# Moving two steps of the output path of a groupnorm-attention kernel: VectorE's block transpose from slot 1 to slot 5, GpSimd's residual add from slot 5 to slot 7

## The chip, the cores and the metric

The kernel runs on one core of a Trainium2 chip. The metric is the device time of one execution in microseconds (us). Before the change it is 1938.38 us, the median of 3 runs (1937.92 to 1938.48).

## What is computed

For each of 4 images x of 256 channels by 4096 positions:

```python
xn   = groupnorm(x)                       # 32 groups of 8 channels, no weights
f, g = Wq @ xn, Wk @ xn                   # 64 x 4096 each
h    = Wv @ xn                            # 256 x 4096
beta = softmax(f.T @ g, axis=0)           # 4096 x 4096, over the rows n
out  = x + gamma[0] * (h @ beta) + xn     # the residual is x + xn
```

## The kernel before, in words

**Stages and slots.** The columns of the softmax matrix are worked off in chunks of 256: 16 chunks an image (CPB), 64 in all (K). One chunk is one stage k of the main loops. Its 4096 rows are 8 groups of 1024, and each group is one slot g. Every engine has its own copy of the loop over `n = 8k + g` (lines 410, 560, 677 and 938), with its part of each slot written out in program order; an engine only ever waits on semaphores, and everything behind a waiting instruction on that engine waits too. j is the number of the stage within its image, 0 to 15.

**A slot.** TensorE, on every second slot, first computes the scores of two groups of the chunk two stages ahead (`scores`, line 456, placed by `SCORES_AT`, line 61), then the 24 matmuls of `weigh` (line 483) that multiply the exponentials PH and PL of this slot with V into the output banks O. ScalarE copies scores to SC (`store`, line 607) and takes exponentials (`exps`, line 616). VectorE keeps running maxima (`maximum`, line 765) and subtracts them from the scores four slots ahead (`subtract`, line 818). GpSimd computes PL, the low half of the exponentials, three slots ahead (`low_weights`, line 375).

**The output path of a chunk.** In slot 0 of the next stage VectorE divides and scales the finished output (`divide`, `scale_output`, lines 845 and 851) into OSB. In slot 1, `turn_blocks` (line 859) transposes OSB in 32 by 32 blocks into OT. The SyncE queue, SP, waits for that in `regroup` (line 270) and issues 16 DMAs that move the blocks to ATT. In slot 5, GpSimd's `add_attention` (line 390) waits for all 16 to land and adds ATT to the residual RES, which `residual` (line 379) made in slot 4. Then SP stores the chunk (line 268).

**The order on SP.** SP works one list in order. For stage k (line 305) it holds: `regroup(k - 1)`; in stage 13 of an image (j == FG_FIRST + 1) six `move_f` and four `double_g` for the next image; in stage 14 `move_f` of unit 7; `store(k - 1)`, which waits for the add; `residual_input(k + 1)`; in some stages an xin load of 1 MB (line 281), with which VectorE later works in slots 3 and 5 (bn_stats in stages 1 to 4, `normalise` in stages 7 to 10); in stage 13 the last `move_f` and three `double_g`. `move_f(u)` (line 283) copies a unit of f and g of the next image into F1 with two DMAs (lines 290, 291), and `double_g(u)` (line 293) copies g into the other half of GG with one (line 297).

**Who needs the moves.** TensorE computes the scores of the next image's first chunk in stage 14. It waits for them in slots 0, 2, 4 and 6 (lines 568 to 572):

```python
                    if i == 0:
                        pe.wait_ge(f_in[q % G], 32 * (nb + 1))
                        pe.wait_ge(f_in[q % G + 1], 32 * (nb + 1))
                    if q % G == 0 and i % 2 == 0:
                        pe.wait_ge(g_in[i // 2], 16 * (nb + 1))
```

So slot 0 needs units 0 and 1 and the doubled unit 0, slot 6 needs units 6 and 7. There are three such changes of image.

Of the kernel before, what the change touches and what calls it, by code (L numbers as in the profile page):

```python
# [5 lines left out]
def groupnorm_attention(nc, x, wqT, wkT, wvT, gamma, out):  # L6
# [66 lines left out]
    with ExitStack() as ctx:  # L73
# [275 lines left out]
        def _(pool):  # L349
# [25 lines left out]
            def low_weights(s):  # L375
                pool.wait_ge(exp_done, s + 1)
                pool.tensor_tensor(PL[:, s % RING, :], sc(s), PH[:, s % RING, :], ALU.subtract).then_inc(pl_ready, 1)  # L377

            def residual(k):
                b = k // CPB  # L380
                pool.wait_ge(res_coefs, b + 1)
                pool.wait_ge(xres_in, 16 * (k + 1))
                if k >= 2:
                    pool.wait_ge(out_stored[k % 2], 16 * (k // 2))
                for h in range(H):
                    r = pool.tensor_scalar(RES[:, k % 2, h, :], xres[:, h, :], rscale[:, b % 2, h:h + 1],
                                           rbias[:, b % 2, h:h + 1], ALU.mult, ALU.add)
                r.then_inc(res_ready, 1)

            def add_attention(k):  # L390
                for q in range(NQ):
                    pool.wait_ge(att_in[q], 16 * NQ * (k + 1))
                pool.wait_ge(res_ready, k + 1)
                flat = "p h m q n -> p (h m q n)"
                r = RES[:, k % 2, :, :].rearrange("p h n -> p (h n)")
                pool.tensor_tensor(r, r, ATT[:, :, :, :, :].rearrange(flat), ALU.add).then_inc(out_ready, 1)  # L396

            def low_input(b, p):
                for h in range(H):
                    pool.wait_ge(xh_ready, H * NFG + H * (NPC * (b - 1) + p) + h + 1)  # L400
                    pool.tensor_tensor(XL[:, h, piece(p)], xin[:, h, :], XH[:, h, piece(p)],
                                       ALU.subtract).then_inc(xl_ready[h], 2)
# [7 lines left out]
            for n in range(K * G):  # L410
                k, g = divmod(n, G)
                b, j = divmod(k, CPB)
                if n + EXP_LEAD < K * G:
                    low_weights(n + EXP_LEAD)
                if g == 4:
                    residual(k)
                if g == 5 and k > 0:
                    add_attention(k - 1)
                if g == 6 and b + 1 < BATCH and NORM_FIRST <= j < NORM_FIRST + NPC:
                    low_input(b + 1, j - NORM_FIRST)  # L420
# [276 lines left out]
        def _(dve):  # L697
# [64 lines left out]
            def normalise(buf, h):  # L762
                return ve.tensor_scalar(buf, buf, nmean[:, h:h + 1], nrstd[:, h:h + 1], ALU.subtract, ALU.mult)

            def maximum(q):

                c, g = divmod(q, G)
                scores = S[:, q % 2, :]  # L770
                dve.wait_ge(s_ready, q + 1)
                if g == 0:
                    return
                if g == 1:
                    dve.wait_ge(s_stored, q)
                    if c > 0:
                        dve.wait_ge(mx_turned, c)
                    ve.tensor_tensor(XM[:, :], scores, sc(q - 1), ALU.max).then_inc(s_maxed, 2)  # L778
                    return
                if q % 2 == 0:  # L780
                    dve.wait_ge(s_stored, q + 1)
                dve.wait_ge(s_maxed, q + 1 if q % 2 == 0 else q - 1)
                ve.tensor_tensor(XM[:, :], scores, XM[:, :], ALU.max).then_inc(s_maxed, 1)  # L783

            def turn_maxima(c):
                dve.wait_ge(s_maxed, G * (c + 1))
                if c > 0:
                    dve.wait_ge(mxq_ready, c)
                ve.transpose(MT[:, :], XM[:, :]).then_inc(mx_turned, 1)
# [14 lines left out]
            def column_maxima(c, o):  # L804

                dve.wait_ge(mx_shared, c + 1)
                if c > 0:
                    dve.wait_ge(mb_ready, c)
                ve.tensor_reduce(mxc[:, :], o[:, 0:NQ * NB].rearrange("p (i j) -> p j i", i=NQ), axis=AX.X,
                                 op=ALU.max).then_inc(mxc_ready, 1)  # L810
# [7 lines left out]
            def subtract(s):  # L818
                k = s // G
                dve.wait_ge(mb_ready, k + 1)  # L820
                dve.wait_ge(s_stored, s + 1)
                tile = sc(s).rearrange("p (i m) -> p i m", i=GT)
                ve.tensor_tensor(tile, tile, MB[:, 0:M].unsqueeze(1).to_broadcast([P, GT, M]),  # L823
                                 ALU.subtract).then_inc(sub_ready, 1)
# [20 lines left out]
            def divide(k):  # L845
                dve.wait_ge(weighed, (k + 1) * G)
                for m in range(MB2):
                    r = ve.reciprocal(rden[:, m:m + 1], bank(k, m)[:, C:C + 1])
                r.then_inc(rden_ready, 1)

            def scale_output(k):
                dve.wait_ge(rden_ready, k + 1)
                if k > 0:
                    dve.wait_ge(osb_turned, k)
                for m in range(MB2):
                    ve.tensor_scalar(OSB[:, m, :], bank(k, m)[:, 0:C], rden[:, m:m + 1], gam[:, :],  # L856
                                     ALU.mult, ALU.mult).then_inc(osb_ready, 1)
# [80 lines left out]
            for n in range(K * G):  # L938
                k, g = divmod(n, G)
                b, j = divmod(k, CPB)  # L940
                if g == 0 and k > 0:
                    divide(k - 1)
                    scale_output(k - 1)
                q = SCORES_AT.get(n)
                if q is not None:
                    maximum(q + 1)
                if k > 0 and n + SUB_LEAD < K * G:
                    subtract(n + SUB_LEAD)
                if q is not None:
                    maximum(q)  # L950
                if n == 2:
                    turn_maxima(1)
                    subtract(6)
                    subtract(7)
                    quadrant_maxima(1)
                if n == 4:
                    column_maxima(1, shared0)
                    spread_maxima(1)
                if k == 0:
                    for s in FIRST_SUB[g]:  # L960
                        subtract(s)
                if g == 7 and k + 2 < K:
                    turn_maxima(k + 2)
                if g == 1 and k > 0:
                    turn_blocks(k - 1)
                if g == 1 and 0 < k < K - 1:
                    quadrant_maxima(k + 1)
                if g == 3 and 0 < k < K - 1:
                    column_maxima(k + 1, S[:, 0, :])
                    spread_maxima(k + 1)  # L970
                extra(k, g, MID)
                extra(k, g, END)
                if g in (3, 5) and b + 1 < BATCH:
                    part = g // 2 - 1
                    if STAT_FIRST <= j < STAT_FIRST + NPC:
                        p = j - STAT_FIRST
                        dve.wait_ge(xin_in, 16 * (2 * NPC * b + p + 1))
                        for h in range(H):
                            last = ve.bn_stats(stats[:, h, 2 * p + part, :], xin[:, h, part * 512:(part + 1) * 512])
                        if part == 1:  # L980
                            last.then_inc(xin_read, 1)
                    if NORM_FIRST <= j < NORM_FIRST + NPC:
                        p = j - NORM_FIRST
                        dve.wait_ge(xin_in, 16 * (2 * NPC * b + NPC + p + 1))
                        normalise(xin[:, part, :], part).then_inc(xn_ready, 1)
                if b + 1 < BATCH:
                    if (j, g) == (COEFS_AT, 3):
                        dve.wait_ge(xin_read, (b + 1) * NPC)
                        group_means(b + 1)
                    if (j, g) == (COEFS_AT, 5):  # L990
                        group_variances(b + 1)
                    if (j, g) == (COEFS_AT, 7):
                        guess_roots(b + 1)
                    if (j, g) == (COEFS_AT + 1, 3):
                        finish_roots(b + 1)
                    if (j, g) == (COEFS_AT + 1, 5):
                        spread_coefficients(b + 1)
# [26 lines left out]
```

## Time and profile before

| what | value |
|---|---|
| median of 3 runs | 1938.38 us |
| the profiled execution's own time | 1938.83 us |
| span of its instructions | 1937.0 us |
| TensorE matmuls busy | 1890.4 us (98% of the span) |
| VectorE, ScalarE, GpSimd busy | 1589.5, 1571.4, 1305.3 us |
| mean granted TensorE clock | 0.999 of 2.4 GHz |

The profiled execution takes 1.83 us beyond its span, and 0.45 us more than the median. Times in the trace count from the start of the span. Durations of matmuls overlap, since they are pipelined: the spacing of their starts is their cost.

### The profile page before, as it was taken

How to read it: one execution, taken by the hardware profiler on the slowest of the kernel's cores; microseconds unless marked ns; L12 is line 12 of the kernel's file. 1: busy time of each engine (PE TensorE's matmuls, PEld its weight loads, DVE VectorE, ACT ScalarE, POOL GpSimd, SP SyncE). 2: the span in 40 equal slices, each digit the busy share in tenths (PEclk: the TensorE clock that was granted, in tenths of full speed). 3: DMA queues.
4: the chain of work that ended last, by engine and by line, in shares of the span. 5: the costliest groups of instructions: out<-in, count | busy, mean ns of one | idle time of the engine just before them, and what ended most of it. 6: DMA issues, size and time to landing. Idle time of an engine off the chain costs nothing. (4 is left out here: it accounts for less than half of the span.)

```text
span 1937.0 us, 44170 instructions
## 1 busy us (share of the span) xinstructions
PE 1890.4 (98%) x17476; PEld 1562.9 (81%) x17476; DVE 1589.5 (82%) x1932; ACT 1571.4 (81%) x1677; POOL 1305.3 (67%) x761
## 2 busy tenths in 40 slices
PE   5999999999999999999999999999999999999998
PEld 3678888878878888887887888888788888888887
DVE  7888998877768899987876889998777787888784
ACT  4788889977768888897876888898787788888885
POOL 4367668866646677886654776788565577766777
PEclk9999999999999999999999999999999999999999
DMA  4022112212111211211211211121130011111111
GB/s 143 4 67 77 45 33 74 55 23 67 29 46 49 74 53 29 72 53 31 60 35 39 78 45 54 53 55 45 28 78 18 21 31 33 31 26 31 32 34 34
DMA packets 199021, 91.18 MB, mean 47 GB/s; under 512 B 150176, under 2 KB 191392, under 8 KB 198816
## 3 DMA queue, kind: packets, MB, share of 16 engines
q1 hardware_dynamic: 198816, 88.36, 17.4%
q8 instruction: 139, 2.28, 0.5%
q14 instruction: 66, 0.54, 0.1%
HBM read 46.60 MB, written 16.78 MB: 33 GB/s over the span
## 5 line engine op out<-in xcount | busy, mean ns | idle before, releaser
L377 POOL TENSOR_TENSOR PL<-SC,PH 128x1024 f16<-128x1024 f32 x511 | 1088.8, 2137 | 572.2 <-ACT SC L621 568.1
L492 PE MATMUL O<-V,PH 128*128 128x257 f16 x4096 | 1119.1, 273 | 4.3 <-DVE OSB L856 3.1
L494 PE MATMUL O<-V,PL 128*128 128x257 f16 x4096 | 1119.0, 273 | 0.0
L493 PE MATMUL O<-V,PH 128*128 128x256 f16 x4096 | 1117.2, 273 | 0.0
L620 ACT ACTIVATE PH<-SC 128x1024 f16<-128x1024 f32 x511 | 539.1, 1055 | 123.1 <-PE O L494 116.8
L823 DVE TENSOR_TENSOR SC<-SC,MB 128x1024 f32<-128x1024 f32 x511 | 613.6, 1211 | 0.1
L614 ACT ACTIVATE SC<-S 128x1024 f32<-128x1024 f32 x512 | 502.0, 1012 | 115.4 <-issue 102.0
L783 DVE TENSOR_TENSOR XM<-S,XM 128x1024 f32<-128x1024 f32 x384 | 468.4, 1220 | 127.4 <-PE S L480 126.1
L621 ACT ACTIVATE SC<-SC 128x1024 f32<-128x1024 f32 x511 | 533.0, 1043 | 0.0
L492 PEld LDWEIGHTS O<-V,PH 128*128 128x128 f16 x4096 | 406.3, 99 | 53.9 <-DVE OSB L856 4.4
L493 PEld LDWEIGHTS O<-V,PH 128*128 128x128 f16 x4096 | 401.1, 98 | 50.2
L494 PEld LDWEIGHTS O<-V,PL 128*128 128x128 f16 x4096 | 401.0, 98 | 50.1
L474 PE MATMUL S<-GG,F 128*128 128x256 f16 x1024 | 154.3, 273 | 6.1 <-ACT SC L614 2.5
L480 PE MATMUL S<-GG,F 128*128 128x256 f16 x1024 | 156.4, 275 | 0.0
L477 PE MATMUL S<-GG,F 64*128 64x256 f16 x2048 | 156.3, 272 | 0.0
L778 DVE TENSOR_TENSOR XM<-S,SC 128x1024 f32<-128x1024 f32 x64 | 78.4, 1224 | 87.3 <-ACT SC L614 87.2
L480 PEld LDWEIGHTS S<-GG,F 128*128 128x128 f16 x1024 | 79.2, 98 | 59.9 <-issue 54.0
L477 PEld LDWEIGHTS S<-GG,F 64*128 64x128 f16 x2048 | 79.1, 94 | 59.8 <-issue 53.9
L474 PEld LDWEIGHTS S<-GG,F 128*128 128x128 f16 x1024 | 98.9, 98 | 24.1 <-issue 6.5
L834 DVE TENSOR_TENSOR V<-O,V 128x512 f16<-128x512 f32 x62 | 42.4, 689 | 59.3 <-ACT V L631 59.0
L631 ACT CAST V<-O 128x512 f16<-128x512 f32 x62 | 35.9, 586 | 61.9 <-PE O L453 61.6
L396 POOL TENSOR_TENSOR RES<-RES,ATT 128x512 f32<-128x512 f32 x63 | 80.5, 1278 | 0.4 <-DMA ATT<-OT 0.4
(106 smaller groups left out, 1100.8 us busy)
## 6 DMA issues: line engine op xcount, KB each, us to landing
xin<-x SPq DMA_DIRECT2D x24, 1024.0 KB, 5.6
xres<-x SPq DMA_DIRECT2D x64, 256.0 KB, 2.8
out<-RES SPq DMA_DIRECT2D x64, 256.0 KB, 2.2
ATT<-OT SPq DMA_DIRECT2D x1008, 16.0 KB, 1.9
F<-GG SPq DMA_DIRECT2D x64, 64.0 KB, 2.0
GG<-GG SPq DMA_DIRECT2D x32, 128.0 KB, 2.4
SC<-x SPq DMA_DIRECT2D x3, 1024.0 KB, 7.3
SC<-x SPq DMA_DIRECT2D x2, 512.0 KB, 10.5
```

The lines of the kernel that those rows point to most:

```text
L377: pool.tensor_tensor(PL[:, s % RING, :], sc(s), PH[:, s % RING, :], ALU.subtract).then_inc(pl_ready, 1)
L474: mm(to(a, i), F1[:, rows(a, i)], G1[:, cols], start=True, stop=False)
L477: mm(to(a, i), F1[half, rows(a, i)], GL[half, cols], start=i % 2 == 1, stop=i % 2 == 0)
L480: m = mm(to(a, i), F1[:, rows(a, i)], G1[:, cols], start=False, stop=True)
L492: mm(o[:, 0:C + 1], PH[:, n % RING, cols], vh, start=t == 0, stop=False)
L493: mm(o[:, 0:C], PH[:, n % RING, cols], vl, start=False, stop=False)
L494: w = mm(o[:, 0:C + 1], PL[:, n % RING, cols], vh, start=False, stop=t == T - 1)
L614: nc.scalar.activation(sc(q), S[:, q % 2, :], ACT.Copy).then_inc(s_stored, 1)
L620: nc.scalar.activation(PH[:, s % RING, :], sc(s), ACT.Exp, bias=SHIFT)
L621: nc.scalar.activation(sc(s), sc(s), ACT.Exp, bias=SHIFT).then_inc(exp_done, 1)
L783: ve.tensor_tensor(XM[:, :], scores, XM[:, :], ALU.max).then_inc(s_maxed, 1)
L823: ve.tensor_tensor(tile, tile, MB[:, 0:M].unsqueeze(1).to_broadcast([P, GT, M]), ALU.subtract).then_inc(sub_ready, 1)
```

## The change

VectorE's `turn_blocks(k - 1)` stands in slot 5 of the stage in place of slot 1, behind that slot's `subtract`. GpSimd's `add_attention(k - 1)` stands in slot 7 in place of slot 5, behind that slot's `low_weights`. Nothing else differs; SP's list is the same text.

```diff
@@ gpsimd: for n in range(K * G)
                 if g == 4:
                     residual(k)
-                if g == 5 and k > 0:
+                if g == 7 and k > 0:
                     add_attention(k - 1)
@@ vector: for n in range(K * G)
                 if g == 7 and k + 2 < K:
                     turn_maxima(k + 2)
-                if g == 1 and k > 0:
+                if g == 5 and k > 0:
                     turn_blocks(k - 1)
                 if g == 1 and 0 < k < K - 1:
                     quadrant_maxima(k + 1)
```

## Rows read from the trace of the kernel before

**Rows 1.** The page's first part: busy time of each engine.

```profile
PE 1890.4 (98%) x17476; PEld 1562.9 (81%) x17476; DVE 1589.5 (82%) x1932; ACT 1571.4 (81%) x1677; POOL 1305.3 (67%) x761
```

**Rows 2.** Waits of PE: line, releaser, total us, times, longest us.

```profile
PE O L451 <- DVE V L834: 5.0, 15, 0.9
```

**Rows 3.** Timeline of VectorE, stage 14 of the first image: start us, us.

```profile
483.14 0.70 DVE L864 STREAM_TRANSPOSE OT<-OSB 128x512 f32<-128x512 f32 x1
...
491.93 1.22 DVE L783 TENSOR_TENSOR XM<-S,XM 128x1024 f32<-128x1024 f32 x1 [1.64 <-PE S L480]
...
495.34 1.21 DVE L823 TENSOR_TENSOR SC<-SC,MB 128x1024 f32<-128x1024 f32 x1
```

**Rows 4.** Timeline of the SP queue, stages 13 and 14 of the first image.

```profile
454.73 10.26 SPq L277 DMA_DIRECT2D ATT<-OT  x16
...
470.75 1.29 SPq L297 DMA_DIRECT2D GG<-GG  x2
...
483.87 10.63 SPq L277 DMA_DIRECT2D ATT<-OT  x16
...
495.19 0.60 SPq L291 DMA_DIRECT2D F<-GG  x1
```

**Rows 5.** Timeline of PE: first scores of slots 0 and 6, stage 14.

```profile
475.94 0.60 PE L474 MATMUL S<-GG,F 128*128 128x256 f16 x4
...
497.32 0.60 PE L474 MATMUL S<-GG,F 128*128 128x256 f16 x4 [0.15 <-issue]
...
1424.53 0.60 PE L474 MATMUL S<-GG,F 128*128 128x256 f16 x4
...
1446.77 0.60 PE L474 MATMUL S<-GG,F 128*128 128x256 f16 x4 [1.01 <-issue]
```

**Rows 6.** Timeline of the SP queue at the third change of image.

```profile
1419.92 2.33 SPq L297 DMA_DIRECT2D GG<-GG  x2
...
1444.64 0.60 SPq L291 DMA_DIRECT2D F<-GG  x1
```

**Rows 7.** Landing of line 297's DMAs, from its source view.

```profile
DMA to landing us min/median/max: 2.3/2.4/3.4
```

**Rows 8.** Timeline of PE at its first matmuls; then engine windows: length, busy, PEclk.

```profile
23.73 0.58 PE L436 MATMUL S<-XH,wqkh 128*128 128x512 f16 x1 [23.73 <-ACT XH L648]
...
27.60 0.59 PE L441 MATMUL S<-XL,wqkh 128*128 128x512 f16 x2
28.03 0.27 PE L451 MATMUL O<-wvh,XH 128*128 128x256 f16 x1
...
73.00:74.00 1.00, 1.00 (x6) 0.69 (x5) 1.00 (x1) 1.00 (x3) 0.87 (x1) 0.50 0.00 0
```

**Rows 9.** Timeline of a plain stage (61) and of the last: VectorE, PE, SP, GpSimd.

```profile
1852.77 1.21 DVE L823 TENSOR_TENSOR SC<-SC,MB 128x1024 f32<-128x1024 f32 x1
...
1868.01 0.60 PE L474 MATMUL S<-GG,F 128*128 128x256 f16 x4
...
1914.39 10.60 SPq L277 DMA_DIRECT2D ATT<-OT  x16
...
1926.45 1.26 POOL L396 TENSOR_TENSOR RES<-RES,ATT 128x512 f32<-128x512 f32 x1 [0.36 <-DMA ATT<-OT]
...
1933.37 0.69 DVE L870 TENSOR_TENSOR RES<-O,RES 128x512 f32<-128x512 f32 x1 [0.82 <-PE O L508]
```

**Rows 10.** The page's groups: GpSimd's low halves of the exponentials.

```profile
L377 POOL TENSOR_TENSOR PL<-SC,PH 128x1024 f16<-128x1024 f32 x511 | 1088.8, 2137 | 572.2 <-ACT SC L621 568.1
```

**Rows 11.** Landing of line 281's loads; timelines of PE and VectorE in stage 8.

```profile
DMA to landing us min/median/max: 5.0/5.6/7.2
...
307.95 0.60 PE L474 MATMUL S<-GG,F 128*128 128x256 f16 x4
...
315.01 2.28 DVE L763 TENSOR_SCALAR xin<-xin,nmean,nrstd 128x1024 f32<-128x1024 f32 x1
```

## The prediction

> **What bounds the kernel now.** I began with the page's first part: TensorE is busy for 1890.4 of 1937.0 us [rows 1]. So nothing that another engine saves can bring much; the question is only where TensorE would have to wait. The view of waits shows how little it waits now: its largest wait inside the stages is on VectorE's low half of V (line 834), 5.0 us in 15 waits, up to 0.9 each [rows 2]. Next I read SP's timeline, because both edits release work there. One `regroup` is 16 issues of about 0.65 us: 10.26 and 10.63 us in the two stages shown [rows 4]. Everything behind it on SP waits for VectorE's turn and for these 10 us. That matters at two stages of an image, 13 and 14, where the moves of the next image's f and g stand behind `regroup`.
>
> TensorE needs the moves at once. In stage 14 the last F1 copy (line 291) was issued at 495.19 and the scores of slot 6 began at 497.32, 2.13 us later, after 0.15 us idle that no compute engine ended [rows 4, 5]. At the third change of image the same pair is 1444.64 and 1446.77: again 2.13 us, with 1.01 us idle [rows 5, 6]. The second has the same 2.13. So this wait is already last at all three changes of image: whatever delays unit 7's move delays the end.
>
> **Part 1: the turn moves by 13.4 us.** In stage 14 the turn began at 483.14. In slot 5 it stands behind the subtract that began at 495.34 and took 1.21, so it begins at 496.55, 13.41 us later [rows 3]. It can't run ahead: slot 4's maximum, ahead of it in VectorE's order, waited for TensorE's scores of slot 4 (491.93) [rows 3]. The pattern of the other two changes of image is the same.
>
> **Part 2: slot 6 of stage 14.** SP starts `regroup` 0.73 us after the turn starts (483.87 against 483.14) [rows 3, 4], then moves unit 7. Nothing in that chain gets shorter, so TensorE's start moves from 497.32 by the turn's shift, 13.4 us. It was already the last to come, so none of that is covered. Three times: **+40.2 us**. While it lasts VectorE, ScalarE and GpSimd run out of scores and give nothing back.
>
> **Part 3: slot 0 of stage 14.** In stage 13 `regroup` moves by the same 13.4 us, and with it six `move_f` and the four `double_g`. Slot 0 wants the first `double_g`: issued at 470.75, landing after a median 2.4, needed at 475.94 [rows 4, 5, 7]. That leaves 2.8 us of cover. New: 470.75 + 13.4 + 2.4 = 486.55, a wait of 10.6 us. The third change of image gives 1419.92 + 13.4 + 2.4 - 1424.53 = 11.2 [rows 5, 6]; the second, by the same working, 11.6. Sum **+33.4 us**. The two stalls of one image add up: after the first, slots 2 and 4 find their units moved, and VectorE reaches slot 5 of stage 14 behind slot 4's scores as before. Below, the moves' own waits could already have cost SP some of its time, about 0.5 us each, so 31; above, 12.5 each with a slower run of issues, 37.
>
> **Part 4: TensorE's clock.** Waits of 10 to 13 us are new here, so I take their price from the rows nearest to them. At its first matmuls, after 23.73 us idle, TensorE took from 23.73 to 27.60 for ten matmuls of 512 columns, where a pair later takes 27.60 to 28.03, 0.215 each [rows 8]. That is 3.87 in place of 2.15 us: 1.7 us lost, at the spacing of 1.2 GHz. A window at 73 us shows a granted clock of 0.50 too, that is 1.2 GHz, after slots in which TensorE had waited [rows 8]. Six stalls at 1.7: **+10.3 us**. Ends: 0, if the clock holds, and 20, if each return takes twice as long.
>
> **Part 5: the add in slot 7, in all stages.** I set the chain against TensorE's need in stage 61. The subtract of slot 5 ends at 1852.77 + 1.21 = 1853.98, so SP starts at 1854.7. In the last stage GpSimd waited for the landings and began its add 12.06 us after SP's start (1926.45 against 1914.39) [rows 9]. So the add starts at 1866.8 and ends near 1868.0. The low half queued behind it takes 2.14 [rows 10] and is done at 1870.2. TensorE wants it in slot 3, after the scores that begin at 1868.01 [rows 9], about 1.5 us of them, and 24 matmuls at 0.11: 1872.1. So GpSimd now waits some 3 us a stage, and TensorE not at all: cost **0**, with only 1.9 us of cover left (1.0 if `regroup` takes 11.5). If that were gone, every stage would pay the excess.
>
> The store and the 1 MB load queue behind this add. The load is issued about 1 us after it, 1869.0, and lands 5.6 later (up to 7.2), at 1874.6. VectorE's `normalise` began 7.06 us after its stage's slot-2 scores (315.01 against 307.95) [rows 11], which in stage 61 to 62 is 1875.1. So the load is just in time or up to 2 us late. A late load delays VectorE in slot 3, then its turn, the add and the next load. Stages 7 to 10 of three images can lose about 1 us an image to that: **+3 us**, between 0 and 8.
>
> **Part 6: what is won, and the tail.** Slot 1 loses 0.70 us of VectorE. Only the waits on line 834 could gain: below 5.0 us in all [rows 2], of which three of up to 0.9 lie in slot 1 behind the turn. But stage 0 of an image also has V work in slot 5, where the turn now stands in front, so I take 0, from -2 to +2. In the last stage VectorE has no maxima to wait for and the turn moves behind two subtracts only, 2.4 us. The last add of GpSimd, at 1926.45, ends near 1930, before VectorE's final add at 1933.37 [rows 9]: 0.
>
> **The sum.** 40.2 + 33.4 + 10.3 + 3 = 86.9 us on the profiled execution's 1938.83, so 2025.7; the median of the runs lies 0.45 lower: **2025 us**, 4.5% slower.
>
> **A rule against the rows.** By the rows one issue on SP costs 0.65 us and 16 of them 10.3 to 10.6 [rows 4], and all sums above use that. The Trainium skill, "DMA: Bandwidth & Descriptors", section "Anatomy of one DMA", gives about 50 ns for a sequencer's dispatch of one DMA (its figures are for GpSimd's path); 16 would be 0.8 us. The trace disagrees, and the measurement decides.
>
> **Rivals.**
>
> A. *The moves are mostly covered.* The wait in slot 0 vanishes, for instance if SP's issues run much faster when no wait is left between them, and the clock is lost three times only: 40.2 + 5.1, so 1984. For it: 2.8 us of cover there now. Against: SP's row of 16 issues in 10.3 us has no wait inside it. 8%.
>
> B. *GpSimd becomes the bound in all stages.* If the landings of ATT come 3 us later than the row of the last stage shows, the low half of slot 0 is about 1 us late in some 60 stages, +60, on top of the forecast: 2085. For it: 1.9 us of cover is little. Against: the chain was measured at 12.06 us. 8%.
>
> C. *Short issues.* If the regroup's issues cost next to nothing, SP would be through `regroup` and unit 7's two copies at 496.55 + 0.73 + 0.9 = 498.2, TensorE would start at 500.3, 3.0 late, three times: 1948. For it only the page's rule above; the rows speak against. 1%.
>
> D. *Not slower: the relief of slot 1 wins.* With the turn out of slot 1, VectorE reaches its low halves of V earlier, and TensorE's 5.0 us of waits on line 834 [rows 2] go: 1933.8 at best. It decides only if the turn's delay at the changes of image is below 5.0 / 3 = 1.7 us, since unit 7's move is last there. The rows say 13.4. The other way to get there is that slot 6 doesn't wait for that move; two starts exactly 2.13 us after an issue speak against. 2%.
>
> **How the numbers follow.** The forecast has 81%. Its own bounds: below 40.2 + 31 + 0 + 0 - 2 = 69, 2008; above 40.2 + 37 + 20 + 8 + 2 = 107, 2046. The range is 2005 to 2048 and leaves out A, B, C and D, 19%. A measurement of this kernel can tell about 0.2%, 3.9 us, from no change. A, B, C and the forecast are all slower by more; D is split between faster and the same.
>
> **What would show it.** In the profile after: two new waits of TensorE at each change of image, of about 11 us ahead of slot 0's scores and 13 us ahead of slot 6's, named "issue" or a DMA into GG or F1, six in all; 16 issues on SP that start just ahead of slot 6; PEclk below 1 behind each; a wait of GpSimd on ATT of about 3 us in most stages, with TensorE's waits on GpSimd near none. The prediction is wrong in its mechanism if TensorE's idle time spreads evenly over the stages, and wrong in its size if the waits of slot 0 are below 8 us.

## The result, and the profile after

The changed kernel takes **2023.66 us** (median of 6 runs, 2020.69 to 2030.04), against 1938.38 before: a ratio of 1.0445, 95% interval 1.0429 to 1.046. The forecast was 2025 in a range of 2005 to 2048. The profiled execution took 2023.74 us with a span of 2022.0, 85.0 more than before.

The page, first and second part, answers to [rows 1]: TensorE is busy for 8 us more and its share falls to 94%. Its clock row falls below 9 in three places, where VectorE and ScalarE fall too.

```profile
PE 1898.3 (94%) x17476; PEld 1566.2 (77%) x17476; DVE 1593.4 (79%) x1932; ACT 1573.4 (78%) x1677; POOL 1313.9 (65%) x761
...
PE   5899999998799999999779999999977999999998
...
PEclk9999999998899999999889999999988999999999
```

The waits of TensorE (line, releaser, total us, times, longest) answer to [rows 2]:

```profile
PE S L474 <- issue: 71.0, 6, 13.5
...
PE S L474 <- DVE XM L783: 4.8, 7, 2.1
...
PE O L451 <- DVE V L834: 3.2, 15, 0.3
...
PE O L492 <- POOL PL L377: 2.2, 2, 1.9
```

The first row is new and holds 71.0 us in exactly six waits. "issue" means that no instruction of an engine ended them. The timeline of SP at the first change of image answers to [rows 4]:

```profile
471.83 10.26 SPq L277 DMA_DIRECT2D ATT<-OT  x16
482.19 0.55 SPq L290 DMA_DIRECT2D F<-GG  x1
...
487.25 1.29 SPq L297 DMA_DIRECT2D GG<-GG  x2
...
513.37 10.69 SPq L277 DMA_DIRECT2D ATT<-OT  x16
524.16 0.54 SPq L290 DMA_DIRECT2D F<-GG  x1
524.74 0.60 SPq L291 DMA_DIRECT2D F<-GG  x1
```

And TensorE's timeline, the first scores of slots 0 and 6 of stage 14 at the three changes of image, as in [rows 5] (499.45 is slot 2):

```profile
489.83 1.01 PE L474 MATMUL S<-GG,F 128*128 128x256 f16 x4 [9.94 <-issue]
...
499.45 0.60 PE L474 MATMUL S<-GG,F 128*128 128x256 f16 x4
...
526.87 1.01 PE L474 MATMUL S<-GG,F 128*128 128x256 f16 x4 [13.53 <-issue]
...
992.42 1.01 PE L474 MATMUL S<-GG,F 128*128 128x256 f16 x4 [10.24 <-issue]
...
1028.69 1.01 PE L474 MATMUL S<-GG,F 128*128 128x256 f16 x4 [13.17 <-issue]
...
1494.63 1.01 PE L474 MATMUL S<-GG,F 128*128 128x256 f16 x4 [10.90 <-issue]
...
1530.67 1.01 PE L474 MATMUL S<-GG,F 128*128 128x256 f16 x4 [13.16 <-issue]
```

Read the two together: the first `double_g` is issued at 487.25 and slot 0 starts 2.58 later; unit 7's second copy is issued at 524.74 and slot 6 starts 2.13 later, the same 2.13 as before. Four scores also take 1.01 us where they took 0.60: the clock is down when TensorE comes back.

**Where the 85 us lie.** I cut both traces at the reciprocal that opens each stage on VectorE (line 848) and took the difference of each stage's length. The 63 lengths sum to +84.8:

| stages | number | change, us |
|---|---|---|
| 14 of the first three images | 3 | +80.0 |
| 8 to 11 of the first three images | 12 | +4.6 |
| 5 of the first three images | 3 | +2.8 |
| 62 | 1 | +2.1 |
| 0 of the last three images | 3 | -1.8 |
| all others | 41 | -3.0 |

In stages 14 the six waits sum to 70.9 and took the place of 1.2, so 69.8 are idle time of TensorE. The other 10.2 are what the lower clock costs, less a little that is won. From the first scores of slot 0 to those of slot 2, and from those of slot 6 to the next, the three changes of image take 11.2 us longer than before. From slot 2 to slot 4 each takes 0.4 less. Windows (length, then busy time of PE, PEld, DVE, ACT, POOL with counts, PEclk, DMA share, GB/s) around the first wait and after the second:

```profile
479.00:482.00 3.00, 0.89 (x5) 0.20 (x2) 1.55 (x6) 2.08 (x3) 1.26 (x1) 1.00 0.16 24
482.00:485.00 3.00, 0.00 (x0) 0.00 (x0) 0.40 (x1) 0.41 (x1) 1.44 (x2) 0.54 0.34 75
...
494.00:495.00 1.00, 1.00 (x7) 0.68 (x6) 1.00 (x2) 0.08 (x1) 0.00 (x0) 0.50 0.96 262
495.00:496.00 1.00, 1.00 (x7) 0.73 (x6) 1.00 (x2) 0.94 (x1) 0.00 (x0) 0.57 0.82 278
...
529.00:530.00 1.00, 1.00 (x6) 0.71 (x5) 0.14 (x1) 0.57 (x1) 0.00 (x0) 0.50 0.00 0
530.00:531.00 1.00, 1.00 (x11) 0.88 (x9) 1.00 (x2) 0.45 (x1) 0.00 (x0) 1.00 0.00 0
```

TensorE resumes at 489.83 and runs at 1.2 GHz until about 495.9; the second time from 526.87 to 530.0.

### The profile page after: what moved, and what is told of

Same layout as the page of the kernel before. It is cut to its first block and busy times, and to the rows that moved or that the text cites. A ratio compares the mean times of both kernels' runs of the same rounds, so it can differ in the third digit from the quotient of the medians.

```text
span 2022.0 us, 44170 instructions
## 1 busy us (share of the span) xinstructions
PE 1898.3 (94%) x17476; PEld 1566.2 (77%) x17476; DVE 1593.4 (79%) x1932; ACT 1573.4 (78%) x1677; POOL 1313.9 (65%) x761
## 5 line engine op out<-in xcount | busy, mean ns | idle before, releaser
L474 PE MATMUL S<-GG,F 128*128 128x256 f16 x1024 | 156.9, 276 | 80.0 <-issue 71.0
L396 POOL TENSOR_TENSOR RES<-RES,ATT 128x512 f32<-128x512 f32 x63 | 80.4, 1276 | 180.7 <-DMA ATT<-OT 180.7
L480 PE MATMUL S<-GG,F 128*128 128x256 f16 x1024 | 158.9, 278 | 0.0
```

What stands on the lines that cost most here:

```text
L474: mm(to(a, i), F1[:, rows(a, i)], G1[:, cols], start=True, stop=False)
L480: m = mm(to(a, i), F1[:, rows(a, i)], G1[:, cols], start=False, stop=True)
```

## The experiments

The theory: the change costs what it delays on SP, the moves of f and g behind `regroup`, and the clock that those waits cost. The main rival: the late add holds GpSimd in every stage and starves TensorE of low halves.

**Which part costs: stages, queue, edits one at a time.** The first kernel puts turn and add back in stages 13 and 14 only.

```diff
-                if g == 5 and k > 0:
+                if g == (1 if b + 1 < BATCH and j in (13, 14) else 5) and k > 0:
                     turn_blocks(k - 1)
-                if g == 7 and k > 0:
+                if g == (5 if b + 1 < BATCH and j in (13, 14) else 7) and k > 0:
                     add_attention(k - 1)
```

> Edit: the kernel after, but in stages 13 and 14 of the first three images the turn stands in slot 1 and the add in slot 5 again; all other stages keep the change. Theory (the moves of f and g stand behind the late regroup on SP): both new waits of TensorE at each change of image go, with the clock they cost; stages 14 return from about 54 us to 27.4. What is left is what the other stages show between the two traces: +4.6 us in stages 8 to 11, +2.8 in the first stage 5, +2.1 in stage 62, about -7 in the rest. So 1938.4 + 2 = 1941, between 1936 and 1945. Rival (the late add on GpSimd starves TensorE in all stages): only 6 of 63 stages are put back, so nine tenths of the 85 us stay, about 2015.

Measured: 1940.4 (10 runs, 1935.2 to 1942.8), ratio 1.0005 (0.9996 to 1.0015). All but about 2 us are gone with six stages put back, while GpSimd still waits for ATT in 57 stages, 172.2 us in all. The rival is out.

The second leaves VectorE and GpSimd as changed and reorders SP alone:

```diff
                 if k > 0:
-                    regroup(k - 1)
                     if j == FG_FIRST + 1 and b + 1 < BATCH:
...
                     if j == FG_FIRST + 2 and b + 1 < BATCH:
                         move_f((b + 1) * NFG + 7)
+                    regroup(k - 1)
                     store(k - 1)
```

> Edit: the kernel after, with one change on SP: in stages 13 and 14 the move_f and double_g that stood behind regroup stand ahead of it. VectorE and GpSimd keep the change in every stage. Theory: in stage 13 the moves wait only for scores of slots 0 to 4 and are out before the turn, in stage 14 unit 7 is moved at once; all six waits go, also the 0.15 and 1.01 us that TensorE waited for unit 7 before. 1940, between 1935 and 1944, so about 1 below the kernel with two stages put back. Rival (the turn and the add in the two stages cost by themselves, through VectorE's and GpSimd's order, and not through SP's): stages 14 stay near 54 us and the time near 2020.

Measured: 1936.8 (10 runs, 1935.2 to 1943.6), ratio 0.9994 (0.9985 to 1.0004). So it is SP's order: with the turn and the add as late as in the changed kernel, each stage 14 takes 26.7 us in place of 54. None of the six waits is left, nor the two of before the change (0.15 and 1.01 us).

The third moves the add alone (`g == 5` to `g == 7` in GpSimd's loop, the turn in slot 1):

> Edit: the kernel before, with the add alone in slot 7; the turn stays in slot 1. Theory: regroup stays early, GpSimd waits for nothing, the moves on SP are ahead of the store as before. The store and the load behind the add are issued some 6 us later than before, still 10 us ahead of their use. 1938.4, within 2 us. Rival (the later add, with the store and the 1 MB loads behind it, is a cost of its own): +5 us or more, in stages 8 to 11.

Measured: 1938.7, ratio 1.0 (0.9991 to 1.001). The add and what stands behind it on SP cost nothing by themselves. The fourth moves the turn alone (`g == 1` to `g == 5` in VectorE's loop, the add in slot 5):

> Edit: the kernel before, with the turn alone in slot 5; the add stays in slot 5. Theory: GpSimd reaches the add about 22.4 us into a stage and the blocks land near 33, so it waits 10 us or more in every stage, and the low half of slot 6 that stands behind it is done at 36.4 where TensorE wants it at 31.6: about 5 us a stage, 60 stages, +300, and the 80 us of the changes of image on top: 2300, between 2180 and 2400. Rival (GpSimd's stall is covered by the three slots of lead that the low halves have): no more than the change as a whole, about 2024.

Measured: 2354.0 in one run. Its waits of GpSimd and TensorE:

```profile
POOL RES L396 <- DMA ATT<-OT: 641.7, 62, 11.5
```

```profile
PE O L492 <- POOL PL L377: 241.7, 60, 5.6
PE S L474 <- issue: 71.6, 6, 13.6
```

Here is what the second edit is for: without it GpSimd waits over 10 us in each stage, which the low halves' lead doesn't cover, and TensorE waits 4 us of that. A plain stage takes about 6.6 us longer. A part of what exceeds the wait is the clock, which falls in nearly every stage, as one window of stage 7 shows:

```profile
316.00:318.00 2.00, 2.00 (x11) 1.42 (x10) 0.00 (x0) 2.00 (x3) 2.00 (x2) 0.50 0.01 2
```

The 71.6 us on SP's moves are there unchanged: the two costs are separate.

**The dose.** The fifth has the turn in slot 3 (`g == 5` to `g == 3` in the changed kernel):

> Edit: the kernel after, with the turn in slot 3 in place of slot 5, the add in slot 7. Theory (each change of image costs what the turn is late, minus the cover of slot 0): the turn comes about 6.1 us later than before in place of 13.4. Slot 6 of stage 14 waits 6 us, three times 18; slot 0, with 2.8, 1.8 and 2.2 us of cover, 3.3, 4.3 and 3.9, together 11.5; the clock at most 1.7 each, 5 to 10; the relief of slot 1 gives 5 back. 1938.4 + 18 + 11.5 + 7 - 5 = 1970, between 1962 and 1976. Rival (the cost goes with GpSimd's wait in all stages): that wait of about 3 us is gone here, so the time falls to that of before, 1934 to 1940.

Measured: 1980.1, ratio 1.0212 (1.0198 to 1.0226), outside what was expected. Its waits of TensorE:

```profile
PE S L474 <- issue: 29.3, 6, 6.3
```

The six waits came out as worked out, 29.3 against 29.5. What was wrong is the rest. Stages 14 are 39.4 us longer in all, which leaves 39.4 - (29.3 - 1.2) = 11.3 for the clock, nearly 1.9 a wait, though the short ones are of 3.5 us only. And the relief of slot 1 is there in the stages 0 alone (0.6 each): plain stages take 27.48 in place of 27.42. In slot 3 the turn stands ahead of the last two steps of the maxima, which is the likely reason. The clock's price is the same after short waits: from slot 0 to slot 2 TensorE takes 9.55, 9.38 and 9.39 us here after waits of 3.5 to 3.9, and 9.62, 9.22 and 9.00 in the changed kernel after waits of 10 to 11.

**The clock.** In the sixth TensorE has work inside its waits, needless matmuls into a bank that is written afresh later:

```diff
+                if j == FG_FIRST + 2 and b + 1 < BATCH and g in (0, 6):
+                    pe.wait_ge(osb_ready, MB2 * k)
+                    for _ in range(65 if g == 0 else 105):
+                        mm(spare(k)[:, 0:C], wvh[:, 0, 0:P], wvh[:, 0, :], start=True, stop=True)
                 if q is not None:
                     nb, i = divmod(q // G, CPB)
```

> Edit: the kernel after, in which TensorE does 65 and 105 needless matmuls of 256 columns into the spare bank ahead of the scores of slots 0 and 6 of stage 14, 7 and 11.5 us of work inside its waits of 10 and 13 us. Theory (about 10 us of the 85 are the clock: it falls to 1.2 GHz in each wait and stays there for a while after it): the granted clock stays at 2.4 GHz through them, stages 14 shorten by 3.6 us each, 10 us in all, 2013.5, between 2011 and 2017. Rival (the 10 us beyond TensorE's idle time are the refilling of the pipeline of scores, maxima and exponentials, not the clock): no change, 2023.7, or slower.

Measured: 2016.1 (4 runs, 2011.5 to 2017.5), ratio 1.0394 (1.038 to 1.0408), 7.6 below the changed kernel. At the first change of image 2.65 us were left idle ahead of the scores at 520.71, and the clock fell after that although TensorE was busy again:

```profile
518.00:521.00 3.00, 0.35 (x4) 0.29 (x4) 0.00 (x0) 0.00 (x0) 0.00 (x0) 1.00 0.23 52
521.00:524.00 3.00, 3.00 (x22) 1.94 (x21) 1.23 (x2) 1.02 (x1) 0.00 (x0) 0.65 0.00 0
524.00:527.00 3.00, 3.00 (x24) 2.41 (x22) 3.00 (x3) 1.23 (x2) 0.00 (x0) 0.78 0.00 0
```

From there to the next scores it took 8.45 us. At the other two changes it took 6.79, with the clock at 1.00, although the second had 2.71 us of idle time in the same place:

```profile
1022.07 0.60 PE L474 MATMUL S<-GG,F 128*128 128x256 f16 x4 [2.71 <-issue]
```

```profile
1022.00:1025.00 3.00, 2.93 (x29) 2.31 (x30) 1.21 (x2) 1.02 (x1) 0.00 (x0) 1.00 0.00 0
```

The tenth has 120 in place of 105. What I wrote ahead of it, that e6 lost about 1 us at each change of image, holds for the first alone (1.7 us):

> Edit: e6 with 120 needless matmuls ahead of slot 6 in place of 105, so that no idle time of 2.65 us is left behind them. Theory: in e6 the granted clock still fell after that idle time (0.65 and 0.78 in the two windows after it) and cost about 1 us at each change of image; now it doesn't: 3 us less than e6's 2016.1, 2013, between 2009 and 2015. Rival (the clock was no cost in slot 6, e6's gain came from slot 0 alone): the same as e6 within 1 us.

Measured: 2011.6 (4 runs, 2009.9 to 2014.3), ratio 1.0378 (1.0363 to 1.0392), 12 below the changed kernel. Ahead of the first slot 0 the matmuls had to wait 2.6 us for VectorE's OSB, and in the profile the clock fell there, but it was up again when the scores came, and behind slot 6 it stayed up:

```profile
481.00:484.00 3.00, 2.38 (x12) 1.70 (x13) 0.56 (x2) 0.56 (x1) 1.29 (x2) 0.58 0.30 66
...
527.00:530.00 3.00, 3.00 (x30) 2.68 (x28) 3.00 (x3) 2.14 (x3) 0.00 (x0) 1.00 0.00 0
```

```profile
490.29 0.60 PE L474 MATMUL S<-GG,F 128*128 128x256 f16 x4
...
497.08 0.60 PE L474 MATMUL S<-GG,F 128*128 128x256 f16 x4
```

That needless work makes the kernel faster shows that the clock is a cost of its own. Its size is read from like stretches: slot 0 to slot 2, and slot 6 to the next scores, take 6.79 us each in e10's trace, in the changed kernel's 9.62 and 8.21 at the first change; over the three changes that is 11.6 us. The times of the runs are no exact measure of it. The needless work holds up the scores of slots 0 and 6, so that stages 14 are only 6.8 us shorter in all than in the changed kernel (6.9 in e6). And the step from e6 to e10 isn't shown: their four runs each overlap, and the profiled one of e10 (2014.32) is slower than that of e6 (2011.54).

**Is SP's order good by itself?** The seventh gives SP's order of e2 to the kernel before:

> Edit: the kernel before (turn in slot 1, add in slot 5), with SP's order of e2: move_f and double_g ahead of regroup in stages 13 and 14. Theory: before the change unit 7's copy was already last at slot 6 of stage 14; that wait, 0.15 and 1.01 us in the profile, goes. But in stage 13 the moves wait for the scores of slot 4, and regroup behind them starts 10 us later, so the add of slot 5 waits for its blocks once an image and a low half comes late, up to 3 us each. 1938.8, between 1937 and 1946. Rival (SP's order is worth most of what e8 and e9 gained): 1933 or less.

Measured: 1946.6, ratio 1.0044 (1.003 to 1.0058), just above what was expected (1937 to 1946). The moves wait for the scores of slot 4, `regroup` behind them; GpSimd's add of slot 5 waits 9.5 us for its blocks, once an image:

```profile
478.76 1.27 POOL L396 TENSOR_TENSOR RES<-RES,ATT 128x512 f32<-128x512 f32 x1 [9.54 <-DMA ATT<-OT]
```

Stages 14 are 7.4 us longer, of which 6.3 are waits on low halves. So that order pays only with the late turn.

**The smaller terms.** The eighth starts from e2, puts the 1 MB load on SP ahead of the store that waits for the late add, and restores the old slots in the last two stages (`k >= K - 2`). `next_load` holds the loads and waits of lines 322 to 337, which go from their old place:

```diff
                     regroup(k - 1)
+                    if b + 1 < BATCH:
+                        next_load(b, j)
                     store(k - 1)
```

> Edit: the kernel with the moves first (e2), and on SP the 1 MB load of a stage ahead of the store that waits for the late add, and in the last two stages turn and add in slots 1 and 5 again. Theory: the load is issued some 3 us earlier, so VectorE's normalise in slot 3 waits for it no more: stages 8 to 11 lose their +4.6 us; stage 62 its +2.1. What stays is +2.8 in the first stage 5 in some executions, where two tiny VectorE copies were each held until a GpSimd instruction ended, and the relief of slot 1, about -6. 1931, between 1929 and 1934. Rival (stages 8 to 11 are long because GpSimd is late with its low halves, not for the load): they stay at +4.6, 1935.

Measured: 1933.0 (7 runs), ratio 0.9971 (0.9961 to 0.9982). Stages 8 to 11 went from +4.6 to -1.4, so their cost was the load. Stage 62 kept its +1.7: GpSimd's wait in stage 61 is still there, 4.47 us, followed by five low halves without a gap.

```profile
1887.05 1.28 POOL L402 TENSOR_TENSOR RES<-RES,ATT 128x512 f32<-128x512 f32 x1 [4.47 <-DMA ATT<-OT]
1888.28 10.52 POOL L383 TENSOR_TENSOR PL<-SC,PH 128x1024 f16<-128x1024 f32 x5
```

The ninth is e8 with the old slots in stage 4 as well, the eleventh is e9 with the last three stages (`k >= K - 3`) in place of two. VectorE's line of the ninth is shown; GpSimd's has 5 and 7 in place of 1 and 5.

```diff
-                if g == (1 if k >= K - 2 else 5) and k > 0:
+                if g == (1 if k >= K - 2 or (b + 1 < BATCH and j == COEFS_AT - 1) else 5) and k > 0:
```

> Edit: e8, with turn and add in slots 1 and 5 again in stage 4 of the first three images as well. Theory (the +2.8 us of stage 5 come from GpSimd's backlog after its wait for the add in stage 4: it runs its low halves without a gap, and each copy of 2 elements on VectorE waits for the end of the one running): without the wait there is no backlog, stage 5 stays at 29.96 or below, and the executions spread less; 1930, between 1928 and 1932, and about 1 below e8. Rival (the long copies are chance and have nothing to do with GpSimd's order): the same median as e8 within 0.5 us.

> Edit: e9, with the last three stages in place of two in the old slots. Theory (the +2.1 us of stage 62 come from stage 61, whose late add holds GpSimd for 4.5 us just ahead of a stage of 21 us, in which the low halves have no time to catch up): stage 62 returns to 20.9 us and the time falls by 2: 1929.4, between 1928 and 1931, against 1931.4 for e9. Rival (the short stage is long for VectorE's order): the same as e9 within 0.5 us.

Measured: 1931.4 (5 runs), ratio 0.9964 (0.9951 to 0.9978), and **1929.4** (5 runs, 1929.1 to 1929.5), ratio 0.9952 (0.9939 to 0.9964). Stages 5 sum to 0.0 against before in both, where e8 had +1.2; e9's median is 1.6 below e8's, but a few runs of each spread by 2 to 5 us, so that step alone is not beyond its noise. Stage 62 returns to 20.94 in e11. This last kernel is faster than the changed one and the one before, by 0.48% against before, with an interval that is clear of no change.

## Why the prediction was right

**What bounds the kernel, and part 1.** The turn of stage 14 began at 512.64 with slot 4's scores at 506.38, 6.3 us behind; before it stood 7.1 ahead of them (483.14, and 490.21 in the trace of before). That is a shift of 13.3, forecast 13.4.

```profile
512.64 0.70 DVE L864 STREAM_TRANSPOSE OT<-OSB 128x512 f32<-128x512 f32 x1
```

**Part 2 (slot 6, forecast +40.2).** Waits of 13.53, 13.17 and 13.16, 39.9, less the 1.2 that were there: **38.7**.

**Part 3 (slot 0, forecast +33.4).** Waits of 9.94, 10.24 and 10.90, **31.1**, at the lower bound given. From SP's start to the first `double_g` it took 15.4 us (471.83 to 487.25) in place of 16.0: the moves' own waits had cost some of that, as the bound allowed.

**Part 4 (clock, forecast +10.3).** **10.2** net by the trace: 11.2 lost, 1.3 won from slot 2 to slot 4, and 0.3 elsewhere in stages 14. That the clock is a cost is shown by e6 and e10. The 1.7 a wait is a mean of unlike parts, though: between the first scores of slots 0 and 2 TensorE now takes 9.62 us (489.83 to 499.45) against 6.92, so 2.7 are lost there (2.3 and 2.1 at the other changes), and 1.3 to 1.4 behind slot 6. That the price fitted is in part luck. It was taken from ten matmuls, most of them spaced 0.43 us for 512 columns, which is the spacing of 1.2 GHz, but the record of the granted clock reads 1.00 there, which the prediction didn't say:

```profile
24.00:25.00 1.00, 1.00 (x4) 0.33 (x3) 0.96 (x3) 1.00 (x3) 1.00 (x2) 1.00 0.00 0
```

**Part 5 (all stages, forecast 0, and +3 for the loads).** GpSimd waits 180.7 us in 60 stages, 3.0 on average, as forecast, and TensorE's wait on low halves is 2.2 us in all. But the cover was thinner than the 1.9 us that were worked out: the wait varies from 0.7 to 5.0 us, and in stage 61, after one of 4.8, the low half of slot 3 was done 0.9 us ahead of TensorE's matmuls with it, in stages 8 to 11 0.1 to 1.8 us ahead (3.2 before). Rival B was nearer than its 8% says. The loads cost **4.6**: VectorE waited for xin 11.5 us in 8 waits at line 763. One of them in stage 8 of the first image, and its load on SP:

```profile
312.59 0.49 SPq L281 DMA_DIRECT2D xin<-x  x1
```

```profile
319.54 1.00 DVE L763 TENSOR_SCALAR xin<-xin,nmean,nrstd 128x1024 f32<-128x1024 f32 x1 [2.39 <-DMA xin<-x]
```

VectorE also waited 6.6 us in 7 waits at line 979, its bn_stats of stages 1 to 4, which the prediction left out; these twelve stages are still 0.8 us shorter in all than before.

What part 5 missed is stage 62, **+2.1**. "TensorE not at all" held for stages of 27.4 us; the last two have no scores and take 21, so the 1.9 us of cover that I worked out for stage 61 isn't what a short stage has. TensorE's one long wait on a low half is there:

```profile
1981.57 0.28 PE L492 MATMUL O<-V,PH 128*128 128x257 f16 x1 [1.91 <-POOL PL L377]
```

**Part 6 (forecast 0).** The relief of slot 1 was real: **-4.8**, in stages 0 (0.6 each) and 0.12 in nearly every plain stage. I looked for it only on line 834, whose waits fell from 5.0 to 3.2 us. The other place is the stretch from slot 2 to slot 4: in stage 61 TensorE took 7.06 us for it before, and takes 6.94 now. `share_maxima` stands there and waits for VectorE's last maximum of slot 2. Counted from slot 2's scores that maximum ended at 5.43 us before and ends at 5.22 now, and `share_maxima` began at 5.53 and begins at 5.48. No view has a wait there, so that this is the place is likely and not shown. So rival D's mechanism exists, at 5 us against 80.

Missed altogether: stage 5 of the first image, **+2.8**, below.

The sum: 38.7 + 31.1 + 10.2 + 4.6 + 2.1 + 2.8 - 4.8 = 84.7, against 86.9 forecast. Parts 2 and 3, which rest on the mechanism, came within 4% and 8%. That the sum is only 2.2 us off is luck besides: the terms that I got too high (2 and 3, by 3.8) and the relief that I left out (4.8) stand against what I missed (2.1 and 2.8) and the loads (1.6 too low).

**The rivals.** A: both waits came, so no. B: e1 and e2 rule it out, and its margin was thin (part 5). C: an issue took 0.64 us (16 in 10.26). The Trainium skill's "DMA: Bandwidth & Descriptors", section "Anatomy of one DMA", has about 50 ns for a dispatch, in a table for GpSimd's path; for these issues on SP the trace again shows another cost, and it decides. D: its mechanism is there and far too small.

## What to carry to other kernels

A step that is moved takes its whole queue along: before moving one, list what stands behind it on SP and who needs that next, and don't look only at its own consumer. Here one transpose of 0.7 us was given 13 us of freedom, and the 16 DMAs behind it held up other transfers of each image, of which the first `double_g` had 2.8 us or less to spare and unit 7's copies none. If a late step is wanted, first move out of its way in the queue what doesn't depend on it: with that alone, the same two edits turned from 4.5% slower to the time of before (e2), and with the loads moved too and six stages put back to 0.5% faster (e11).

## What the runs showed that I had not expected

**Two-element copies of 2.1 us.** In stage 5 of the first image, the timelines of VectorE and GpSimd in the changed kernel:

```profile
231.46 2.11 DVE L714 COPY cm<-mv 128x2 f32<-128x2 f32 x1
233.49 2.17 DVE L715 COPY cv<-mv 128x2 f32<-128x2 f32 x1
```

```profile
229.33 6.31 POOL L377 TENSOR_TENSOR PL<-SC,PH 128x1024 f16<-128x1024 f32 x3
235.63 1.08 POOL L386 TENSOR_SCALAR RES<-xres,rscale,rbias 128x256 f32<-128x256 f32 x2
```

The three low halves end near 231.4, 233.5 and 235.6, and the copies near 233.6 and 235.7. Each copy ends when one of GpSimd's instructions does; in that stage line 714 took 1.16 before and line 715 0.16. The Trainium skill has a rule that fits in "SBUF — State Buffer", section "Who interferes with whom": VectorE's copies can take a port pair that is shared with GpSimd and held for a whole instruction. The trace agrees. GpSimd's backlog after its wait for the add, low halves without a gap, makes such a hold likely, and TensorE then waited 2.10 us on line 783. In the other two images the same stage was hardly longer (0.0 and +0.1), with copies of 1.37 and 0.16, 0.24 and 2.18 us, so it is a matter of phase. In e9 and e11, with stage 4 in its old slots, the copies take 1.37 to 1.38 and 0.16 us in all three images and stages 5 are as long as before. Whether the long ones are also a part of the larger spread of the changed kernels isn't shown.

**The clock after short waits.** Waits of 3.5 us cost as much clock as waits of 10 (e5). Shorter ones went either way: in e6 the granted clock fell after 2.65 us of idle time, when TensorE was already busy again, and stayed at 1.00 after 2.71 us at the next change of image. What decides that, no run here shows.
